# Attention with its row maxima in four parts per image and its score products in half-row tiles

## What is computed

```python
x = x + conv(groupnorm(x))                       # stage 1, prepare()
t = tokens(x)                                    # (16, 3136, 32)
h = layernorm(t)
q, k, v = h @ Wq + bq, h @ Wk + bk, h @ Wv + bv
t = t + softmax(q @ k.T / sqrt(32)) @ v + h      # stage 2, attend(): 3136 x 3136 scores per image
t = t + mixture_of_experts(layernorm(t))         # stage 3, finish()
```

## Time and profile before

| | us |
|---|---|
| median of 3 runs | 3082.78 |
| lowest, highest | 3080.33, 3083.63 |
| the profiled execution, its own time | 3085.89 |
| span of the profiled execution | 3084.1 |
| PE, DVE, ACT, POOL busy in it | 2487.4, 2402.0, 1653.8, 273.4 |
| mean granted clock of TensorE | 0.868 |

### The profile page before, as it was taken

How to read it: one execution, slowest core, us unless ns; L and a number is a source line. 1 busy time by engine, 2 the same in 40 slices (tenths; PEclk the granted TensorE clock), 3 DMA queues, 4 the chain that set the end, 5 groups by cost and what they waited for, 6 DMA issues and landing times. The chain is left out here.

```text
span 3084.1 us, 48223 instructions
## 1 busy us (share of the span) xinstructions
PE 2487.4 (81%) x18582; PEld 995.0 (32%) x18582; DVE 2402.0 (78%) x4213; ACT 1653.8 (54%) x2170; POOL 273.4 (9%) x260
## 2 busy tenths in 40 slices
PE   1846467483469999999999999999999994877786
PEld 0423132231012222222222222222222224766664
DVE  4455546455899999999999999999999803888887
ACT  0233243334027777777777777777777791333332
POOL 0000000000000000000000000000000000545455
PEclk9978778785569999999999999999999995666666
DMA  5585765813200111011101110110110003122220
GB/s 129 116 197 151 178 160 155 209 70 152 69 1 1 53 53 54 1 53 54 53 2 54 53 36 18 53 53 14 40 53 22 4 19 131 64 71 88 70 87 21
DMA packets 55030, 220.95 MB, mean 72 GB/s; under 512 B 13478, under 2 KB 26402, under 8 KB 46114
## 3 DMA queue, kind: packets, MB, share of 16 engines
q1 hardware_dynamic: 53354, 214.13, 23.9%
q10 hardware_dynamic: 1464, 3.95, 0.4%
HBM read 81.67 MB, written 74.60 MB: 51 GB/s over the span
## 5 line engine op out<-in xcount | busy, mean ns | idle before, releaser
L1027 DVE TENSOR_REDUCE at_XM<-at_psX 128x1 f32<-128x448 f32 x2688 | 1552.4, 620 | 66.6 <-PE at_psX L925 39.4
L995 ACT ACTIVATE at_PR<-at_psS 128x896 f32<-128x896 f32 x1344 | 1159.5, 914 | 368.2 <-PE at_psS L904 365.9
L941 PE MATMUL at_psV<-at_PR,at_V 128*32 128x448 f32 x5376 | 644.4, 551 | 0.5 <-ACT at_PR L995 0.5
L904 PE MATMUL at_psS<-at_US,at_KS 128*128 128x448 f16 x2688 | 629.8, 355 | 2.5 <-ACT at_PR L995 0.9
L925 PE MATMUL at_psX<-at_KS,at_US 64*128 64x448 f16 x1344 | 501.2, 373 | 83.3 <-DVE at_XM L1027 76.6
L925 PE MATMUL at_psX<-at_KS,at_UH 64*128 64x448 f16 x1344 | 501.3, 373 | 0.0
L925 PEld LDWEIGHTS at_psX<-at_KS,at_US 64*128 64x128 f16 x1344 | 125.1, 93 | 750.2 <-DVE at_XM L1027 718.2
L904 PEld LDWEIGHTS at_psS<-at_US,at_KS 128*128 128x128 f16 x2688 | 205.0, 98 | 287.9 <-ACT at_PR L995 140.8
L1327 POOL TENSOR_TENSOR fi_WE<-fi_WE 128x256 f32<-128x256 f32 (+1 forms) x224 | 213.0, 980 | 172.5 <-DVE fi_WE L1381 171.6
L1333 POOL TENSOR_TENSOR fi_T<-fi_T,fi_RES 128x800 f32<-128x800 f32 x16 | 30.0, 1875 | 1918.1 <-DVE fi_T L1396 1918.1
L326 PE MATMUL psA<-sb_stacks,sb_lhs 128*32 128x448 f32 x1568 | 174.2, 574 | 23.5 <-DMA sb_stacks<-sb_T 10.5
(11 more groups left out here) (185 smaller groups left out, 2060.6 us busy)
## 6 DMA issues: line engine op xcount, KB each, us to landing
sb_stacks<-sb_Xp SPq DMA_DIRECT2D x64, 496.8 KB, 12.3
sb_stacks<-sb_T SPq DMA_DIRECT2D x64, 443.0 KB, 8.1
sums<-at_O SPq DMA_DIRECT2D x16, 1568.0 KB, 6.2
fi_SUMS<-sums SPq DMA_DIRECT2D x16, 1568.0 KB, 6.6
at_KS<-key_stacks SPq DMA_DIRECT2D x16, 784.0 KB, 7.8
at_US<-query_stacks SPq DMA_DIRECT2D x16, 784.0 KB, 9.6
key_stacks<-sb_KS SPq DMA_DIRECT2D x13, 784.0 KB, 3.9
query_stacks<-sb_YU SPq DMA_DIRECT2D x13, 784.0 KB, 3.6
```

Of the source, the lines that this page charges most:

```text
L904: last = nc.tensor.matmul(psS[:, i % 2, j, 0:TILE], KS[:, b, c * P:(c + 1) * P], US[:, b, t * TILE:(t + 1) * TILE], start=True, stop=True)
L941: last = nc.tensor.matmul(psV[C * q:C * q + C, 0:TILE], V[:, b, G * k + q, :], PR[:, (2 * q4 + q // 2) % PRS, q % 2, :], start=(k == 0), s ...
L995: nc.scalar.activation(PR[:, (i - 2) % PRS], psS[:, i % 2, :, 0:TILE], ACT.Exp).then_inc(p_ready, 1)
L1027: nc.vector.tensor_reduce(o, psX[:, (at + j) % 3, 0:TILE], AX.X, ALU.max).then_inc(x_done, 1)
```

## The change

- An image's maxima are made by parts of 7 key-side chunks of queries (PARTS = 4; the last has 3 and the half chunk): 49 reductions per part. Each part is reduced, transposed, copied and sent to US by itself: four turns per image, not one. The float16 split moves from DVE to POOL.
- 32 pairs of maxima (LEAD) come before the first scores, not 98; the last 15 steps have none and one has one. Steps are 42 per image, of which two have three pairs. The half chunk's scores and EXP come in four, at every 12th step, instead of all at an image's start.
- A slot's scores are four products of 64 rows, in two rounds: rows 0 to 63 of the first chunk beside rows 64 to 127 of the second, then the other halves, added in PSUM. PE waits on a semaphore, `s_half`, between the rounds, and a pair of maxima stands between them.
- A step is now: first round, pair of maxima, second round, sums of two steps back, first round, pair, second round (and a third pair, where there is one).
- The last half chunk's values are padded with zeros to 128 rows, so that its sums are in tiles of 128 x 32. PR has 8 buffers, not 6.

```diff
+        PARTS = 4
+        PC = 2 * TILE // P
+        LEAD = 32
+        LAG = 2
...
+        def turn_place(m, p):
+            if p < PARTS - 1:
+                return place(m, last_pair(p) + 1) + 2
+            return place(m + 1, 0) + 2 if m + 1 < N else place(m, XPAIRS - 1) + 2
...
+        def pairs_of(n, s):
+            q = n * STEPS + s
+            a, z = (min(LEAD + k * XPAIRS // STEPS, N * XPAIRS) for k in (q, q + 1))
+            return [divmod(g, XPAIRS) for g in range(a, z)]
...
+            sp.wait_ge(zeroed, 1)
             for n in range(B):
                 load(n)
-            max_rows(0)
             for n in range(N):
-                if n + 1 < N:
-                    max_rows(n + 1)
-                store(n)
...
+                for p in range(PARTS):
+                    max_rows(n, p)
+                    if p == 1 and n >= 1:
+                        store(n - 1)
...
+            def half_scores(n, p):
+                b, at = n % B, half_slot(n, p)
+                pe.wait_ge(m_in, rows_in(n, p))
...
+            def scores(n, s, i, j):
+                b, at, (t, c) = n % B, slot(n, s, i), divmod(2 * s + i, NF // 2)
+                if j == 0 and at >= 2:
+                    pe.wait_ge(p_ready, at - 1)
+                if j == 1:
+                    pe.wait_ge(s_half, 2 * (n * 2 * STEPS + 2 * s + i) + 2)
+                for h, k in enumerate((j, 1 - j)):
+                    a = HALF * h
+                    last = nc.tensor.matmul(psS[:, at % 2, k, 0:TILE], KS[a:a + HALF, b, (2 * c + k) * P:(2 * c + k + 1) * P],
+                                            US[a:a + HALF, b, t * TILE:(t + 1) * TILE], start=(j == 0), stop=(j == 1))
+                    if j == 0:
+                        last.then_inc(s_half, 1)
...
+            def turn_max(m, p):
+                at = turn_place(m, p)
                 pe.wait_ge(x_done, at - 2)
-                pe.wait_ge(negm_ready, 2 * m + 2)
-                nc.tensor.transpose(psX[0:NC, at % 3, 0:P], negm[:], ident[:]).then_inc(x_full, 1)
+                pe.wait_ge(negm_ready, turned_parts(m, p))
+                nc.tensor.transpose(psX[0:chunks_of(p), at % 3, 0:P], negm[:, p, 0:chunks_of(p)], ident[:]).then_inc(x_full, 1)
...
                 for s in range(STEPS):
...
+                    pairs = pairs_of(n, s)
+                    if s % PSTEPS == 0:
+                        half_scores(n, s // PSTEPS)
+                    scores(n, s, 0, 0)
+                    if len(pairs) >= 1:
+                        maxima(*pairs[0])
+                    scores(n, s, 0, 1)
+                    q = n * STEPS + s - LAG
+                    if q >= 0:
+                        sums(*divmod(q, STEPS))
+                    scores(n, s, 1, 0)
+                    if len(pairs) >= 2:
+                        maxima(*pairs[1])
+                    scores(n, s, 1, 1)
+                    if len(pairs) >= 3:
+                        maxima(*pairs[2])
...
+        @block.gpsimd
+        def _(pool):
+            def rows(m, p):
+                k = m * PARTS + p
+                h, a = chunks_of(p), k % 2
+                pool.wait_ge(x_done, turn_place(m, p) + 1)
...
+                nc.gpsimd.tensor_copy(mrow[0:h, a, 0], mt[0:h, a]).then_inc(order, 1)
+                pool.wait_ge(order, k + 1)
+                nc.gpsimd.tensor_tensor(mrow[0:h, a, 1], mt[0:h, a], mrow[0:h, a, 0], ALU.subtract).then_inc(mrow_ready, 1)
```

More of the change, by code:

```diff
@@ L827, in attend, with chunks_of @@
         o_out = [sem(f"o_out{b}") for b in range(B)]
         block = ctx.enter_context(nc.Block())
[L831 to L838, removed]
+        LC = NF - (PARTS - 1) * PC
+        def chunks_of(p):
+            return PC if p < PARTS - 1 else LC + 1
@@ new lines, in unit, with last_pair, place @@
+        def unit(u):
+            p = min(u // (PC * NT), PARTS - 1)
+            t, j = divmod(u - p * PC * NT, PC if p < PARTS - 1 else LC)
+            return (PC * p + j, t) if t < NT else (NF, u - NF * NT)
+        def last_pair(p):
+            return ((p + 1) * PC * NT - 1) // 2 if p < PARTS - 1 else XPAIRS - 1
+        def place(m, i):
+            return (m * (UNITS + PARTS) + 2 * i + sum(last_pair(p) + 1 < i for p in range(PARTS - 1))
+                    - (m >= 1 and i == 0))
+        def turn_place(m, p):
+            if p < PARTS - 1:
+                return place(m, last_pair(p) + 1) + 2
+            return place(m + 1, 0) + 2 if m + 1 < N else place(m, XPAIRS - 1) + 2
@@ new lines, in ends_at, with turns_at, turned_parts @@
+        def ends_at(m, i):
+            return [(m, p) for p in range(PARTS) if last_pair(p) == i]
+        def turns_at(m, i):
+            t = [(m, p) for p in range(PARTS - 1) if last_pair(p) + 1 == i]
+            if i == 0 and m >= 1:
+                t.append((m - 1, PARTS - 1))
+            if i == XPAIRS - 1 and m == N - 1:
+                t.append((m, PARTS - 1))
+            return t
+        def turned_parts(m, p):
+            return m * (PARTS + 1) + (p + 1 if p < PARTS - 1 else PARTS + 1)
@@ L848, in turns, with rows_in @@
-        def turns(n, s):
-            return s + AHEAD == STEPS and n + 1 < N
+        def rows_in(n, p):
+            return 16 * (n * ROWS + (2 * (p + 1) if p < PARTS - 1 else ROWS))
         @block.sync
@@ L908, in maxima @@
-            def maxima(m, pair):
-                b, at = m % B, place(m, pair)
-                if pair == 0:
+                for h, t in enumerate(half_tiles(p)):
+                    last = nc.tensor.matmul(psS[HALF * h:HALF * h + HALF, at % 2, 0, 0:TILE], KS[:, b, TF:T],
+                                            US[:, b, t * TILE:(t + 1) * TILE], start=True, stop=True)
+                last.then_inc(s_full, 1)
+            def scores(n, s, i, j):
[10 more added lines that the diff above has]
+                        last.then_inc(s_half, 1)
+                if j == 1:
+                    last.then_inc(s_full, 1)
@@ L911, in maxima @@
+            def maxima(m, i):
+                b, at = m % B, place(m, i)
+                if i == 0:
                     pe.wait_ge(k_in[b], 16 * LOADS * (m // B + 1))
@@ L970, in _ @@
-            scores(0, 0)
-            scores(0, 1)
+            pe.wait_ge(c_in, 16)
+            for m, i in first_pairs():
+                maxima(m, i)
             for n in range(N):
                 for s in range(STEPS):
[L974 to L982, removed]
+                    pairs = pairs_of(n, s)
[14 more added lines that the diff above has]
+                        maxima(*pairs[2])
@@ L984, in _, with half_exponentials @@
+            for q in range(N * STEPS - LAG, N * STEPS):
+                sums(*divmod(q, STEPS))
         @block.scalar
         def _(act):
[L986 to L987 removed]
+            def half_exponentials(n, p):
+                at = half_slot(n, p)
                 act.wait_ge(s_full, at + 1)
[L989 to L995, removed]
+                if n >= 1:
+                    act.wait_ge(v_full, (n - 1) * NT + min(2 * p + 2, NT))
+                nc.scalar.activation(PL[:, p], psS[:, at % 2, 0, 0:TILE], ACT.Exp).then_inc(p_ready, 1)
@@ L1016, in _, with maxima @@
         @block.vector
         def _(dve):
-            def maxima(m, pair):
-                at = place(m, pair)
+            def maxima(m, i):
+                at = place(m, i)
+                for p in range(PARTS):
+                    if m >= 1 and i == p * PC * NT // 2:
+                        dve.wait_ge(negm_ready, turned_parts(m - 1, p))
                 for j in range(2):
+                    c, t = unit(2 * i + j)
                     dve.wait_ge(x_full, at + j + 1)
[L1022 to L1026, removed]
-                    nc.vector.tensor_reduce(o, psX[:, (at + j) % 3, 0:TILE], AX.X, ALU.max).then_inc(x_done, 1)
@@ L1049, in step @@
-            def step(n, s):
-                pairs = pairs_of(n, s)
-                if turns(n, s):
-                    max_parts(n + 1)
-                    dve.wait_ge(negm_ready, 2 * n + 4)
-                if pairs:
-                    maxima(*pairs[0])
-                if turns(n, s):
-                    max_halves(n + 1)
-                if pairs:
-                    maxima(*pairs[1])
-            for pair in range(XPAIRS):
-                maxima(0, pair)
-            for s in range(STEPS - AHEAD, STEPS):
-                step(-1, s)
+                    o = XE[:, t:t + 1] if c == NF else XM[:, t, c:c + 1]
@@ L1065, in _ @@
+            nc.vector.memset(V[HALF:P, :, NF], 0.0)
+            nc.vector.memset(V[0:HALF, :, NC], 0.0).then_inc(zeroed, 1)
+            for m, i in first_pairs():
+                maxima(m, i)
             for n in range(N):
                 for s in range(STEPS):
-                    step(n, s)
+                    for m, i in pairs_of(n, s):
+                        maxima(m, i)
 def finish(nc, wts, scr, out):
```

183 lines of the change are left out of this document (92 added, 91 removed).

## The result

The changed kernel takes **3278.83 us** (median of 4 runs), the kernel before 3082.83: ratio 1.0635, 95% interval 1.0616 to 1.0653. It is 196 us slower; I had forecast 155, with a range that holds the result. The stage runs from 772.9 to 2741.3 us in the new trace, 1968.4 us against 1773.6, so 195 us of the 196 are in it.

A forecast was written before the change was run, and what follows sets the result against it. PE was taken to bound the steady step of 2.34 us. The stage's terms, mainly 656 steps of 2.65 us (1738.4), summed to 1928.5 us against 1773.6, +155, giving 3238 us; range 3105 to 3345.

The forecast's parts named there:

- A: Steady step: the PE-DVE round trip of the maxima sets it, 2.65 us for 2.34; 3238 us in all, 61%.
- B: Steady step: the pairs of maxima keep DVE full and it alone sets the pace; 2969 us, 11%.
- C: Steady step: no 0.10 us drain between half-row tiles and the sums, step 2.45 us; 3107 us, 8%.
- D: Score rounds: weight loads of half-row tiles are not hidden, +0.19 us a step; 3362 us, 12%.
- E: Clock: PE idles enough to get 1.2 GHz throughout, about +1000 us; 3%.
- F: Rows of US: the shorter lead is not enough and rows come late, +200 us; 3440 us, 3%.
- Half chunk ... Nothing: Step's start: half chunk's products and tiling changes make 0.96 us, under the pairs' 1.08, so cost nothing.
- ahead of the first scores: Stretch before scores at 1.2 GHz: 32 pairs 40.6 us and a turn 1.0; DVE's memset adds 0.5.
- keeps, 109: Longer interval: padded half chunk's sums, without a tiling change before them, add 0.23 us each, 25.1 in all.
- turns without sums between, 47: Turns at a step's second or third pair: add 0.54, 0.74 or 0.90 us each.
- turns with the sums, 15: Turns at a step's first pair: PE's 2.25 us falls into the full path, +0.98 us each.
- behind the last maxima: Last 15.5 steps, s_half without cover: 2.2 us each, and 3.5 for last sums and keeps; 37.5 us.

The follow-up runs named there:

- e1: Changed kernel with the second pair of maxima directly behind the sums, ahead of the slot's first round: 3177.96 us, ratio 1.030.
- e3: Changed kernel with its reductions over 224 of the 448 columns only: 3098.82 us, ratio 1.0043.
- e9: Changed kernel with all four half-row rounds in one block ahead of the first pair and the half chunk behind the sums: 3070.75 us, ratio 0.9951.
- e4: Kernel before the change with its reductions over 224 of the 448 columns only: 3044.73 us, ratio 0.9872.
- e5: Changed kernel with the half chunk's scores between the sums and the second slot's first round: 3260.86 us, ratio 1.0574.

## Why the prediction was right, and where it was short

**Right.** The forecast was A, that the round trip of the earlier trace rows takes over, and the trace has its two intervals as the prediction put them, 1.57 and 1.08 against 1.573 and 1.069. e1 shortens the one by a round, e3 the other by a piece of DVE's work, and each leaves its counterpart alone to 0.01 us; e9 brings the sums' interval to the 1.17 that is left when both rounds go. The two intervals are moved separately, so the step's mechanism is shown, not only argued. What bounded the kernel before is shown too: in e4 DVE's busy time is 819 of the 1400 us from 1000 on, for 1349 before, and the step does not move. Those 1349 us, 96%, are no sign of a full DVE: a reduction is 0.62 long, but the next one starts 0.54 after it where no wait lies between (four take 2.23 above), so a pair needs 1.08 of the 1.17 us it has.

**B** (DVE kept full) did not come: DVE waits 247 us of 1400 for PE. Its price was wrong as well: 1344 x 1.16 is 1559 and not 1554, and by the 1.08 just given, and not 1.16, it would have been some 108 us lower still. **C** (no 0.10 between half-row tiles and the sums) is out: the sums begin 0.29 after a round starts, which enters in 0.19. **D** is out: in the step's timeline a round starts 0.20 behind a pair (2013.24 to 2013.44), and a pair 0.20 behind a round, where D wanted 0.28. The Trainium skill (TensorE: Matmul & The Clock Gate, Part 3, on what overlaps and what doesn't) says that a load overlaps running products only in another row group. This trace disagrees, as the full tiles of the earlier trace rows had. **E** (lower clock throughout) did not come: 1.00 in the window from 1000 to 2600 us at 88% busy. But five short falls behind turns cost 6 us, which the sum has at nothing. **F**: no wait for rows of US. (The prediction's 0.98 us for a POOL operation of 128 x 256 is the mean of all shapes on that line; the median in the earlier trace rows is 0.74.)

**Short by 40 us in the stage** (1928.5 forecast, 1968.4 measured). The step that failed is "Half chunk ... Nothing". I had compared PE's work, 0.96 us, with the 1.08 of the pairs, and put its EXP on ACT's idle time. But the half chunk is a slot of psS like any other, and there are two: the first round behind it needs the slot that was filled 0.29 us before. Measured, 47 intervals of 1.83 for 1.07 and 0.06 on the round behind: 39 us, and e5 shows that it is the slot. That this is nearly the whole of the 40 is luck: the other terms miss by up to 7 us each, in both directions, and come near to cancelling. Forecast and measured:

| term | forecast | measured, by the counted intervals |
|---|---|---|
| ahead of the first scores | 41.6 + 0.5 | 40.5 (772.9 to 813.4) |
| keeps, 109 | 0.23 each | 0.19 each (1.766 for 1.573) |
| turns without sums between, 47 | 0.54 to 0.90 | 0.67 (mean 1.74) |
| turns with the sums, 15 | 0.98 | 0.92 (2.49) |
| half chunks | 0 | 39 |
| 656 steps | 2.65 each | 2.64 each, 5 us less in all |
| lower clock behind five turns | 0 | 6 |
| behind the last maxima | 37.5 | 44.2 (2697.1 to 2741.3) |

In the last row the steps are 2.28 for 2.2, and a half chunk there meets the same slot: 1.2 us for each of the two. The rest is the last of the 64 turns, which the sum leaves out. PE stands still for 1.64 us ahead of its transposing at 2699.14, the next scores come some 2 us late, and then the granted clock is 0.56 from 2699.1 to 2703.0 us.

## What to carry to other kernels

Two engines that hand a buffer back and forth have a round trip with a fixed length, and it bites only where the producer's other work between two hand-overs is shorter. Before work is moved, write down the interval between the hand-overs on both sides of it: here PE's work in a step fell by 0.2 us and the step grew by 0.3, because one interval became so long that DVE ran dry, and the other had so little work of PE's in it that PE had to wait for DVE. And whatever passes through a shared buffer takes a turn in it, however small it is: ask which turn the next one must then wait for.

## What the runs showed of the hardware

A product of 64 rows took 356 ns and entered in 0.19 us, as one of 128 rows did (355 ns), and two on different halves of the rows ran beside each other, in rounds as in pairs of maxima. A change of tiling cost the same 0.10 us in every order tried, and none was to be seen between two blocks of half-row products. The granted clock stayed at the upper level though PE stood still for about 0.26 us in every step. It fell to the lower one for a few us (0.56 over 3.9 us) behind 5 of the 16 turns in which PE stood still for 0.52, 0.54 and 0.41 us in short order, and behind the last turn, with 1.64 us at a stretch. A reduction of 128 x 448 float32 from PSUM takes 0.62 us alone, and the next one starts 0.54 after it.
